# Second attention in another order, and the turned maxima split by products with plus and minus identity

## The reference

```python
x = x + _L0_xattn_ref(_layernorm(x), ctx_1024, ctx_1024, ...)
x = x + _L0_ffn_ref(_layernorm(x), ...)
x = x + _L1_xattn_ref(_layernorm(x), ctx_1024, ...)   # 16 heads of 16: softmax(Q K^T / 4) V, then Wo
x = x + _L1_ffn_ref(_layernorm(x), ...)
```

## Time and profile before

| | us |
|---|---|
| time, median of 3 runs | 716.63 (713.95 to 716.72) |
| the profiled execution | 716.42 |
| its span, first to last instruction | 714.6 |
| PE busy in the span | 678.2 (95%) |
| DVE busy | 519.5 (73%) |
| ACT busy | 359.3 (50%) |
| POOL busy | 334.1 (47%) |
| TensorE clock, mean granted | 0.998 |

### The profile page before, as it was taken

The page is one execution under the profiler, slowest core; times in us unless marked ns, Lnnn a source line. Parts: engine busy times, 40 slices in busy tenths (PEclk is TensorE's granted clock), DMA queues, the critical chain, the costliest instruction groups (busy, mean ns, idle before and its releaser), DMA issues.

```text
span 714.6 us, 16405 instructions
## 1 busy us (share of the span) xinstructions
PE 678.2 (95%) x6471; PEld 571.6 (80%) x6471; DVE 519.5 (73%) x1166; ACT 359.3 (50%) x700; POOL 334.1 (47%) x232
## 2 busy tenths in 40 slices
PE   8899999999999999999889999999997999999998
PEld 5678788875568999999776777777676887999998
DVE  5788888888867554432777888888988686948464
ACT  2222122226865646555658787787877243232323
POOL 2333333426965588773336878878776000000000
PEclk9999999999999999999999999999999999999999
DMA  9979000003882587733896876877720000000000
GB/s 293 351 263 68 27 27 27 28 26 101 228 216 83 163 236 222 225 88 59 154 183 150 177 182 154 186 159 154 161 63 2 2 2 14 1 27 1 26 14 27
DMA packets 67676, 81.57 MB, mean 114 GB/s; under 512 B 32930, under 2 KB 56066, under 8 KB 65266
## 3 DMA queue, kind: packets, MB, share of 16 engines
q1 hardware_dynamic: 64210, 72.68, 41.9%
q0 software_dynamic: 2816, 3.67, 2.9%
q10 hardware_dynamic: 576, 4.19, 1.4%
HBM read 60.45 MB, written 19.31 MB: 112 GB/s over the span
## 4 chain that ended last, share of the span: by engine, by line
PE 63%; DVE 11%; ACT 10%; DMA 6%; issue 6%; POOL 4%; SPq 0%; DVEq 0%; POOLq 0%; ACTq 0%
PE psum L1280 7%; PE psum L1297 6%; PE psum L2582 6%; PE psum L900 6%; ACT probs L1979 5%; PE psum L1738 5%; DMA kparts_d<-kp 4%; PE psum L366 4%; PE psum L2263 3%; PE psum L2276 3%; PE psum L2235 3%; PE psum L2301 3%; PE psum L936 2%; ACT qpk L1969 2%; PE psum L1746 2%
## 5 line engine op out<-in xcount | busy, mean ns | idle before, releaser
L2070 DVE TENSOR_REDUCE mx<-psum 112x2 f32<-112x750 f32 x128 | 113.2, 925 | 8.1 <-PE psum L2235 7.6
L1979 ACT ACTIVATE probs<-psum 125x448 f32<-125x448 f32 x192 | 91.1, 559 | 17.2 <-PE psum L2263 16.6
L1886 POOL TENSOR_TENSOR half_sum<-probs 125x896 f32<-125x896 f32 x30 | 62.5, 2082 | 28.2 <-ACT probs L1979 28.2
L900 PE MATMUL psum<-w_parts,c_parts 128*125 128x512 f32 x282 | 71.2, 403 | 2.8 <-DVE kv L656 2.7
L2263 PE MATMUL psum<-qpk,kpk 128*128 128x112 bf16 x768 | 61.2, 215 | 4.3 <-ACT probs L1979 4.2
L900 PEld LDWEIGHTS psum<-w_parts,c_parts 128*125 128x125 f32 x282 | 51.3, 185 | 17.1 <-DVE kv L656 3.7
L2263 PEld LDWEIGHTS psum<-qpk,kpk 128*128 128x128 bf16 x768 | 46.2, 99 | 23.3 <-issue 7.2
L2235 PE MATMUL psum<-kpk,qpk 96*128 96x375 bf16 x256 | 62.2, 325 | 2.4 <-DVE mx L2070 2.2
L1892 POOL TENSOR_TENSOR tile_sum<-half_sum,probs 125x896 f32<-125x896 f32 x30 | 62.9, 2098 | 2.4
L1580 ACT ACTIVATE ctx_all<-psum,cols 128x448 f32<-128x448 f32 (+1 forms) x40 | 22.4, 561 | 80.8 <-PE psum L1746 80.8
L1552 POOL TENSOR_TENSOR rs<-ve,mhalf 112x4 f32<-112x4 f32 (+1 forms) x5 | 4.4, 889 | 108.0 <-DVE ve L1595 108.0
(11 more groups left out here) (259 smaller groups left out, 1636.6 us busy)
## 6 DMA issues: line engine op xcount, KB each, us to landing
we<-in_we SPq DMA_DIRECT2D x12, 1024.0 KB, 5.8
kparts_d<-kp SPq DMA_DIRECT2D x16, 562.5 KB, 5.0
kpk<-kparts_d SPq DMA_DIRECT2D x32, 281.2 KB, 4.4
ctx_all<-in_ctxT SPq DMA_DIRECT2D x16, 375.0 KB, 5.4
kpk<-kparts_d SPq DMA_DIRECT2D x32, 187.5 KB, 5.2
we<-in_we ACTq DMA_DIRECT2D x4, 1024.0 KB, 13.3
kpk<-kparts_d SPq DMA_DIRECT2D x32, 93.8 KB, 4.1
qparts_d<-qp SPq DMA_DIRECT2D x16, 168.0 KB, 4.0
```

The lines of the kernel that those rows point to most:

```text
L900: ins = pe.matmul(banks[B_KV[t]][0:KT, :], parts_of[:, x, k, t * KT:(t + 1) * KT], w_parts[:, k, w], start=(k == 0 and (x, w) == SPLIT[0]) ...
L1886: pool.tensor_tensor(half_sum[:, m], probs[:, m, 0], probs[:, m, 1], ALU.add)\
L1979: act.activation(probs[:, m, t, g * HU * SQ:(g + 1) * HU * SQ], banks[B_ST[u % 3]][0:KT, 0:HU * SQ], ACT.Exp, scale=SCALE)\
L2070: dve.tensor_reduce(mx[:, n % 2, MAX_AT + 2 * j:MAX_AT + 2 * j + 2], psum[0:SQ, first:first + 2, 0:SK], AX.X, ALU.max)\
```

## The change

- The turn is three products in place of two: one fp32 transpose of the maxima at rows 112 to 127, then a bf16 product of the upper halves of the same fp32 numbers with the identity (every second bf16 of `mx`, placed at rows 96 to 111), and one of the upper halves with minus the identity, placed at rows 112 to 127. `high` on ACT and `shift` on DVE are gone; ACT's three spreads read the turned rows in PSUM with scale -1. The constant `lower` is replaced by `minus_one`.
- Unit 0 of the turned scores waits for all three spreads, not for the first.
- `weigh` and `out_product` are cut in two parts each, `add_up(n, 0)` stands ahead of the turn, `add_up(n-1, 1)` behind unit 3 and not behind unit 0, and the scores stand in other places among the units.
- On DVE `invert_sums` and `normalise` stand together behind maximum 3, and `add_x` behind the first maximum of element n+2.
- On ACT the padding of the values stands behind unit 10, not 8.

The diff, cut:

```diff
@@
-SCORES_AFTER, WEIGH_AFTER = {2: (2,), 3: (3,), 7: (4,), 9: (5, 6), 11: (7,)}, 5
-PAD_AFTER = 8
-INVERT_AT, NORM_AT, TEAM_AT = 2, 4, 3
+PAD_AFTER = 10
+INVERT_AT, TEAM_AT = 4, 3
@@ spread_shift(n), ACT
             act.wait_ge(turn_ps.sem, turn_ps.at(n))
-            if n:
-                act.wait_ge(shift_done.sem, shift_done.at(n - 1))
-            act.activation(high[ROWS:], turned, ACT.Copy).then_inc(high_done.sem, 1)
-            act.wait_ge(shift_done.sem, shift_done.at(n))
             for heads in SPREAD:
                 count = heads.stop - heads.start
-                act.activation(qpk[ROWS:, n % AHEAD, heads], spread(shift[ROWS:], 1, count), ACT.Copy)\
+                act.activation(qpk[ROWS:, n % AHEAD, heads], spread(turned, 1, count), ACT.Copy, scale=-1.0)\
                     .then_inc(spread_done.sem, 1)
@@ DVE, set-up
-        dve.tensor_reduce(lower[ROWS:], identb[ROWS:, ROWS + H:], AX.X, ALU.add).then_inc(lower_done.sem, 1)
+        dve.tensor_scalar(minus_one[:], identb[0:SQ, 0:SQ], -1.0, None, ALU.mult).then_inc(lower_done.sem, 1)
@@ step(n), DVE
             more = n + 1 < B
+            if not more:
+                team_ahead(n)
+                invert_sums(n - 1)
+                normalise(n - 1)
+                team_entry()
+                return
             for j in range(1, H // 2):
                 if j == INVERT_AT:
                     team_ahead(n)
...
+                    if n:
+                        invert_sums(n - 1)
+                        normalise(n - 1)
+                two_max(n + 1, j)
             if n + 2 < B:
                 two_max(n + 2, 0)
-            elif more:
+            if n:
+                add_x(n - 1)
+            if n + 2 == B:
                 team_rows()
@@ shift_turn(n), PE
-            for r in range(SHIFT):
-                ins = pe.matmul(banks[B_ST[0]][:, 0:SQ], mx[:, n % 2, (1 - r) * H:(1 - r) * H + 128],
-                                ident[0:SQ, 0:SQ], start=(r == 0), stop=(r == SHIFT - 1), is_transpose=True)
-            ins.then_inc(turn_ps.sem, 1)
+            s, to = n % 2, banks[B_ST[0]][:, 0:SQ]
+            upper = mx[:].bitcast(BF16)
+            high_rows, low_rows = (slice(2 * at + 1, 2 * (at + 128), 2) for at in (H, 0))
+            pe.matmul(to, mx[:, s, 0:128], ident[0:SQ, 0:SQ], start=True, stop=False, is_transpose=True)
+            pe.matmul(to, upper[:, s, high_rows], identb[0:SQ, 0:SQ], start=False, stop=False)
+            pe.matmul(to, upper[:, s, low_rows], minus_one[:], start=False, stop=True).then_inc(turn_ps.sem, 1)
@@ transposed_scores(n, u), PE
-            if t == 0 and (g == 0 or m == 0):
-                pe.wait_ge(spread_done.sem, spread_done.at(n, 2 * m + g + 1))
+            if u == 0:
+                pe.wait_ge(spread_done.sem, spread_done.at(n))
@@ step(n), PE, the new order (weigh and out_product take a part as last argument)
+            score(n + 1, 2)
+            if n == 0:
+                keep_warm()
+            transposed_scores(n, 0)
+            transposed_scores(n, 1)
+            score(n + 1, 3)
+            transposed_scores(n, 2)
+            if n == 0:
+                keep_warm()
+            transposed_scores(n, 3)
+            if n:
+                add_up(n - 1, 1)
+            for u in range(4, 7):
+                transposed_scores(n, u)
+            score(n + 1, 4)
+            transposed_scores(n, 7)
+            score(n + 1, 5)
...
```

More of the change, by code:

```diff
@@ L2265, in transposed_scores, with weigh @@
             ins.then_inc(st_ps.sem, 1)
[L2267 to L2274, removed]
+        def weigh(n, m, odd):
+            if not odd:
+                pe.wait_ge(exp1_done.sem, exp1_done.at(n, UNITS // KC * (m + 1)))
+                pe.wait_ge(vz_done.sem, vz_done.at(n))
+                if m == 0 and n:
+                    pe.wait_ge(au_done.sem, au_done.at(n - 1))
+            for t in range(NKT):
                 for g in range(4):
                     ins = pe.matmul(banks[B_PV][32 * g:32 * g + 32, m * SQ:(m + 1) * SQ],
[L2277 to L2280, removed]
+                                    vz[:, n % 2, t, 4 * m + g, odd],
+                                    probs[:, m, t, (2 * g + odd) * SQ:(2 * g + odd + 1) * SQ],
+                                    start=(t == 0 and not odd), stop=(t == NKT - 1 and odd == 1),
+                                    tile_position=(0, 32 * g))
+            if odd:
+                ins.then_inc(pv_ps.sem, 1)
         def add_up(n, m):
@@ L2293, in add_up, with out_product @@
                 ins.then_inc(sums_ps.sem, 1)
[L2295 to L2303, removed]
+        def out_product(n, half):
+            if half == 0:
+                pe.wait_ge(au_done.sem, au_done.at(n))
+                if n + 2 < B:
+                    pe.wait_ge(exp1_done.sem, exp1_done.at(n + 1, LAST_IN_PRODUCT + 1))
+            for m in range(KC):
+                ins = pe.matmul(product_of(n)[:, half], au[:, m], wo1[:, m, half * 128:(half + 1) * 128],
+                                start=(m == 0), stop=(m == KC - 1))
+            if half:
+                ins.then_inc(wo1_ps.sem, 1)
         def keep_warm():
@@ L2309, in step @@
         def step(n):
[L2310 to L2315, removed]
-                transposed_scores(n, u)
[L2317 to L2322, removed]
-                if u == 9 and not more:
-                    bias_product()
-                for j in SCORES_AFTER.get(u, ()):
-                    if more:
-                        score(n + 1, j)
-                    if j == WEIGH_AFTER:
-                        weigh(n, 0)
@@ L2338, in step, with last_step @@
             shift_turn(n + 1)
+            weigh(n, 1, 0)
+            if n:
+                out_product(n - 1, 1)
             if n + 2 < B:
                 score(n + 2, 1)
-            add_up(n, 0)
-            weigh(n, 1)
+            weigh(n, 1, 1)
+        def last_step(n):
+            team_turn(pe, 0)
+            for u in range(UNITS):
+                transposed_scores(n, u)
+                if u == 0:
+                    add_up(n - 1, 1)
+                if u == 3:
+                    gates(pe, 0)
+                if u == 6:
+                    out_product(n - 1, 0)
+                    out_product(n - 1, 1)
+                if u == 9:
+                    bias_product()
+                    weigh(n, 0, 0)
+                    weigh(n, 0, 1)
+            marked(pe, 0)
+            weigh(n, 1, 0)
+            weigh(n, 1, 1)
```

48 lines of the change are left out of this document (17 added, 31 removed).

## The result

| | before | after |
|---|---|---|
| median, us (8 runs each, side by side) | 716.46 (712.15 to 718.73) | 723.39 (718.35 to 726.98) |
| ratio of after to before | | 1.0092, interval 1.0058 to 1.0126 |
| profiled execution / its span | 716.42 / 714.6 | 720.58 / 718.8 |
| turn 0 to last turn | 168.00 | 173.88 |
| plain step | 10.97 | 11.20 |

The kernel became slower by about 0.9%, where 1.0% faster was predicted; the time lies outside the range. All times and ratios of this document are of fast executions; one of the six of e3_order_alone, 730.96, was slow and is left out. The starts of the turns, subtracted, place the difference. "Forecast" is the term of the prediction.

A forecast was written before the change was run, and what follows sets the result against it. No engine was taken as full; a ring of waits in the second attention's plain step was the bound. Plain steps of 10.36 us for 10.97 and changes in other steps summed to -7.15: 716.42 to 709.3 us, range 706 to 714.6.

The forecast's parts named there:

- the ring: Plain step of the kernel before: a closed chain of waits, 1.47 of 10.97 us, in which `au` releases the first weighing.
- The walk: One plain step of the new order, timed group by group from the turn: 10.36 us instead of 10.97.
- rival 1: PE in each plain step: four more changes of kind cost 0.1 each, step about 10.74, time 714.6 us; chance 0.17.
- steps 2 to 10: Nine steps of the loop at 10.36 us each: 93.24 instead of 98.94, a gain of 5.70.
- Step 11: The step with the team statistics: they add 1.0 to DVE's time, giving 11.36 us for 11.66, -0.30.
- The turn: Turn on PE: three products taken as 0.20 us, between 0.15 and 0.35 more; the turn's part alone worth about nothing.
- the 3.3 named as a sign of dear spreads: First exponential of a plain step: expected 3.0 us after the turn; past 3.3 would mean dear spreads or strided products.
- Step 0: First step of the loop: score pair 2 delays the filling products, turn 1 at 387.3 instead of 386.67, +0.65.
- The last step: End of the loop: `team_rows` waits behind `add_x`, starting 1.96 us after the turn instead of 1.10, +0.86.
- Rival 4: Clock around 552 us: a second dip gives 710.9 us, no dip 707.7; included in the forecast's 0.68 chance.
- Rival 2: Key rows landing late for the scores: slower than before from 7.25 us, 723.7 at 7.8; chance 0.07 with anything dearer.
- Rival 3: Only the turn moves, since ACT's branch already sets the ring and the new order frees nothing: 716.9 us; chance 0.08.

The follow-up runs named there:

- e3_order_alone: The changed kernel with the old turn put back, so only the new order remains: median 724.75 us, ratio 1.0139 to the kernel before.
- e1: The changed kernel with DVE's team statistics in step 11 moved ahead of maximum 3: step 11 12.27 us, ratio 1.0041 to the kernel before.
- e2: The kernel before with only the new turn, everything else in the old order: plain step 10.95 us, ratio 0.9984 to the kernel before.
- e5: The kernel before with the first adding up moved ahead of score pair 1: plain step 11.21 us, ratio 1.0051 to the kernel before.
- e4: The changed kernel with the weighings and output product uncut, both halves at the first half's place: plain step 11.15 us, ratio 1.0080 to the kernel before.
- e8: The changed kernel with the first adding up right behind the half output product, score pair 0 behind it: plain step 11.16 us, ratio 1.0077 to before.
- e6: The changed kernel with weighing and adding-up groups side by side, no cuts, statistics early: plain step 10.68 us, ratio 0.9993 to the kernel before.
- e9: The grouped, uncut version of the changed kernel, with step 0's filling products ahead of score pair 2: median 715.13 us, ratio 0.9973 to the kernel before.

## Why the prediction was wrong

**The bound.** "No engine is full" was right, and so was the ring with `au` releasing W. The 1.47 of 10.97 us called waiting was not: 0.43 of it was passages that the sum of 9.50 left out, 1.04 was waiting. The new order took about 0.6 of that away.

**The step that failed first: the price of a passage on PE.** The walk charged half a W 0.63, S 0.33, A 0.41, half an O 0.47 and the turn 0.20, wherever they stand, and rival 1 took its 0.03 from W ahead of S or of T, which is the same passage twice and no comparison. The row that prices it stood in the earlier trace rows: S ahead of A was held 0.42 (453.31 to 453.73), S ahead of the turned scores 0.33 (461.41 to 461.74); and A was 0.41 with W behind it, of the same kind. The second A of before and the T0 ahead of it, charged 0.41 and 0.20, stood at 0.53 and 0.30 in the same trace (T0 starts at 455.40):

```profile
455.70 0.59 PE L2289 MATMUL psum<-tile_sum,halves 125*32 125x112 f32 x16
456.23 0.57 PE L2263 MATMUL psum<-qpk,kpk 128*128 128x112 bf16 x8
```

With the measured ones, up to the end of S2: turn +0.14, W +0.08, O +0.06, S +0.09, W +0.08, S +0.01, so 3.05 for the walk's 2.59. From the first W to the turn the walk had 3.68, with 0.15 of waiting in it; it is 4.01. Rival 1 was the right mechanism, with a chance of 0.17 and a price of 0.1; it is about 0.2 for every group of W and A more, three more in a step. That halving O costs the same was not so: 0.49 or 0.53 for half of 0.93. Its time, 714.6, fell short too.

**The step that failed second: what releases W.** The walk put `au` at 6.47 and T9 at 6.68. By its own terms DVE came to 6.62, and with the hand-over to 6.77, so DVE and not ACT was the later already. Measured is 7.19: 6.77, plus the 0.46 by which S2 came late, less 0.04, since S2 had about that to spare in the walk. Thus 10.36 became 11.20: +0.51 ahead of W and +0.33 behind it. With it fell all terms that rest on the plain step: steps 2 to 10 (-5.70 forecast, +2.21 measured), 12, 13 and 14. Step 1 lost an old cost, as said, -0.76 for -1.03.

**Step 11** was the largest miss in one step. The term added the work of the statistics (0.98) and asked for no other engine. Moved behind a later maximum, their last instruction met POOL's sum, which cost 1.30 there and a lower clock behind the wait: +3.47. e1 shows it by taking it away.

**The turn** was right in size: 0.19 ahead of S in e2, with no price of the strided weights; the 0.34 in after is the passage to W. Exponential 0 came 3.44 behind the turn, past the 3.3 named as a sign of dear spreads, but the spreads took 1.77 for 1.88, and it is PE's order that held T0. As a sign it was badly chosen, since it could not tell the two apart. The Trainium skill, "Perfetto Trace Analysis", section "Optimizing Scalar/DVE Operations", had given 0.13 by estimate, and the 0.11 agrees.

**Step 0** came as forecast, +0.64 for +0.65. **The last step**: the team's first turn came 3.84 behind the last turn, as before, not 4.70. The residual started 1.78 behind the turn, forecast 1.50, and `team_rows` 2.12, forecast 1.96, but `team_rows` was shorter (DVE of after, answering to the earlier trace rows, 2.68 before):

```profile
550.64 1.67 DVE L1598 TENSOR_SCALAR ctx_all<-x_all,mv,rs 112x256 f32<-112x256 f32 x2
```

In before they began at 544.17 inside a sum of POOL from 543.88 to 545.97; in after a sum of POOL ended at 551.41, 0.77 behind their start, where it had been 1.80. Behind the end of POOL's sum they took 0.88 before and 0.90 after, the same. So what the longer wait cost came back as a shorter one at the port; no run tested this place by itself. **Rival 4** had the kind right, not the place: one dip stands in step 11, and the dip at 552 is gone, which is the -1.25 of the last stretch. That one need owe nothing to the change: the last stretch of e5 is that of before, has no dip and takes 170.3, where before took 171.5. **Rival 2** didn't happen: key rows land in 5.5 in the median (5.0 in the earlier trace rows), and no plain step waits for them. **Rival 3** was right that the turn earns nothing in a plain step, and wrong in what sets the ring.

## What to carry to other kernels

Before an order of TensorE's groups is changed, count the passages between narrow weight tiles and full ones in a period, and price one from two rows that differ only in what follows: here 0.1 us each way, which made three more groups cost about 0.8 where the shorter waits gave 0.6. Walk every branch of the ring to the end with its last term in it, above all where branches differ by less than an unpriced edit. When an instruction of DVE moves, look at what POOL runs at its new place, however small the instruction is.

## What the runs showed of the hardware

- Groups of 16, 24 or 48 products with weight tiles of 125 by 32, in four positions, cost about 0.1 us more ahead of a group with full tiles, and a full one about 0.1 more ahead of such a group (0.42 for 0.33, 0.58 for 0.49); two narrow groups in a row cost nothing extra. In e5 one more pair made the step 0.24 longer.
- Products that read every second bf16 of an fp32 tile as weights, three in a row with an fp32 transpose, hold PE for 0.19, as two transposes do (e2).
- A Vector instruction on 112 by 2 numbers lasted 1.47 when it started 0.64 into a sum of POOL, and 0.17 with POOL idle (after, before, e1). Three more traces with the same place have 1.46, 1.28 and 1.47 (e3, e4, e8).
- Stretches of about 3.3 us at a granted clock near 0.5, the lower level, stand at 552.0 before and at 508.24 in after, and none in the loop of e1. Behind the stall of step 11 one comes in all four traces that have the stall (after, e3, e4, e8). In the last stretch one comes or stays away with the same order (before, e5) and costs about 1.2. What decides whether one comes was not tested.
- PE stopped for 0.27 to 1.25 in the middle of the same W, with nothing to wait for that the trace shows, in e2, e4, e6 and e9. The cause stays open.
